# Attention and experts on one core: query rows in another order, a wider ring of banks at the end, activation tables loaded ahead

## What is computed

```python
xn = _layernorm(x, axis=-1)
# attention
q = (x @ w_q.T).reshape(B, S, N_HEADS, dk)
k = x @ w_k.T
v = x @ w_v.T
scores = jnp.einsum('bshd,btd->bhst', q, k) * softmax_scale[0]
attn = jax.nn.softmax(scores, axis=-1)
out = jnp.einsum('bhst,btd->bshd', attn, v).reshape(B, S, D)
return out @ w_out.T
# experts, two of eight for each token
t = (x * jax.lax.rsqrt(ms + EPS) * norm_scale).reshape(Bx * Sx, Dx)
h = _swiglu(t @ w1 + b1)
y = h @ w2 + b2
# together
x = x + s * g
```

## Time and profile before

| | us |
|---|---|
| median of 3 runs | 433.36 (432.69 to 433.53) |
| the profiled execution | 432.73 |
| its span in the trace | 430.9 |
| PE busy | 380.3 (88%) |
| DVE busy | 300.6 (70%) |
| ACT busy | 281.7 (65%) |
| POOL busy | 277.9 (64%) |

### The profile page before, as it was taken

How to read it: one execution, slowest core, us unless ns; L and a number is a source line. 1 busy time by engine, 2 the same in 40 slices (tenths; PEclk the granted TensorE clock), 3 DMA queues, 4 the chain that set the end, 5 groups by cost and what they waited for, 6 DMA issues and landing times.

```text
span 430.9 us, 7859 instructions
## 1 busy us (share of the span) xinstructions
PE 380.3 (88%) x2375; PEld 238.9 (55%) x2375; DVE 300.6 (70%) x559; ACT 281.7 (65%) x615; POOL 277.9 (64%) x417
## 2 busy tenths in 40 slices
PE   1787889898989999999569999989979989999994
PEld 1666655343444445444247988878869854444221
DVE  6678888988897788787515756556546648888532
ACT  4854467666777778677525666656646568887893
POOL 6353053538888888888002888888788882577980
PEclk9999569999999999999958999999999999999998
DMA  6321154562222522322615566666756512535211
GB/s 172 99 86 56 73 194 152 208 258 90 73 100 73 172 86 104 99 82 91 146 33 141 176 200 187 175 183 192 203 149 191 151 46 100 183 118 148 58 44 49
DMA packets 51310, 55.40 MB, mean 129 GB/s; under 512 B 11747, under 2 KB 40291, under 8 KB 51142
## 3 DMA queue, kind: packets, MB, share of 16 engines
q1 hardware_dynamic: 46150, 45.45, 35.2%
q0 software_dynamic: 4544, 9.38, 6.2%
q10 hardware_dynamic: 576, 0.08, 0.1%
HBM read 34.46 MB, written 19.95 MB: 126 GB/s over the span
## 4 chain that ended last, share of the span: by engine, by line
PE 49%; DVE 13%; POOL 13%; ACT 9%; issue 7%; DMA 6%; SPq 2%; ACTq 0%; POOLq 0%; DVEq 0%
PE ps L927 12%; PE ps L899 10%; PE ps L914 10%; POOL y_dram L567 10%; DVE neg L1353 6%; PE ps L1063 6%; POOL kvg L569 3%; ACT probs L754 3%; PE ps L876 2%; PE ps L1086 2%; DMA xs<-sorted_dram 2%; DMA y_dram<-early,xs 2%; DMA b_st<-b_col 2%; PE ps L885 1%; PE ps L974 1%
## 5 line engine op out<-in xcount | busy, mean ns | idle before, releaser
L1353 DVE TENSOR_REDUCE neg<-ps 128x4 f32<-128x1024 f32 x128 | 155.3, 1215 | 39.8 <-PE ps L914 39.6
L754 ACT ACTIVATE probs<-ps 128x512 f32<-128x512 f32 x256 | 141.8, 599 | 37.3 <-PE ps L899 35.0
L567 POOL DMA_INDIRECT y_dram<-early,xs x78 | 77.1, 989 | 52.2 <-ACT early L824 31.3
L899 PE MATMUL ps<-qs,k_stack 96*128 96x512 bf16 x256 | 91.4, 384 | 5.1 <-ACT probs L754 3.3
L914 PE MATMUL ps<-k_stack,qs 93*128 93x256 bf16 x512 | 83.0, 287 | 4.3 <-DVE neg L1353 4.2
L1063 PE MATMUL ps<-early,w_st 128*128 128x256 f32 x312 | 78.3, 396 | 8.0 <-DMA b_st<-b_col 5.9
L1429 DVE TENSOR_SCALAR early<-ps,b_st 128x256 f32<-128x256 f32 x78 | 34.2, 480 | 58.8 <-PE ps L1063 47.2
L542 POOL DMA_INDIRECT sorted_dram<-rows,pos_i x64 | 64.7, 1011 | 11.2 <-POOL rows L537 10.3
L1063 PEld LDWEIGHTS ps<-early,w_st 128*128 128x128 f32 x312 | 58.4, 197 | 17.4 <-issue 10.4
L927 PE MATMUL ps<-probs,v_all 128*32 128x512 f32 x512 | 68.1, 605 | 0.0
L914 PEld LDWEIGHTS ps<-k_stack,qs 93*128 93x128 bf16 x512 | 51.6, 103 | 25.2 <-issue 5.4
(11 more groups left out here) (153 smaller groups left out, 422.9 us busy)
## 6 DMA issues: line engine op xcount, KB each, us to landing
w_st<-in_w SPq DMA_DIRECT2D x39, 256.0 KB
qs<-q_dram SPq DMA_DIRECT2D x32, 288.0 KB
sorted_dram<-s_b SPq DMA_DIRECT2D x10, 520.0 KB, 4.7
xs<-sorted_dram SPq DMA_DIRECT2D x39, 130.0 KB, 2.3
early<-y_dram SPq DMA_DIRECT2D x16, 256.0 KB, 4.2
q_dram<-early SPq DMA_DIRECT2D x16, 192.0 KB, 3.7
rows<-in_x SPq DMA_DIRECT2D x8, 256.0 KB
out<-rows SPq DMA_DIRECT2D x16, 128.0 KB, 2.0
```

Source lines behind the costliest of these rows:

```text
L567: gp.indirect_dma_start(out=y_dram, out_offset=bass.IndirectOffsetOnAxis(ap=at[:, t, :], axis=0), in_=ys[:, r, t, :], in_offset=None).then ...
L754: sc.activation(probs[:, u % 2, k, :], ps[:, bank, :], ACT.Exp).then_inc(m["exp_ok"], 1)
L899: te.matmul(ps[:, bank, :], k_stack[0:KALL, at:at + P], qs[0:KALL, u % QS, j * 512:(j + 1) * 512], start=True, stop=True).then_inc(m["exp_ ...
L1353: ve.tensor_reduce(neg[:, b % 2, st, h:h + 4], ps[:, 3 + 2 * (n % 2):5 + 2 * (n % 2), :].rearrange("p a (e t) -> p (a e) t", e=2), AX, ALU ...
```

## The change

- `load_q`: the dimension of the three copies goes behind the 24 rows (`replicated(..., 3, 1)`), so that the three copies of a source row lie in neighbouring partitions. Same bytes, 72 rows of 4 KB.
- `key_rows`: the three parts of a key are written at every third column instead of as blocks of 24.
- `ring`: from step w = 32 on (WIDE_FROM) the ring has seven banks: the four of the maxima and the old three. Its first four items wait until the last maximum has been read (`max_ok` at 128), the next three on the last three items of the old ring, later ones on the item seven before.
- `values(31, 0)` moves from step u = 32 to step u = 31, between `scores_exp(31, 5)` and `project(14)`.
- ACT: a one-column Silu at q = -1, before the first `L817`, and a one-column Exp at q = 39, before the last two blocks are taken out.

```diff
+WIDE_FROM = len(FIRST_ITEMS) + sum(len(ring_items(w)) for w in range(UNITS))
+WIDE_BANKS = (3, 4, 5, 6, WIDE_FROM % 3, (WIDE_FROM + 1) % 3, (WIDE_FROM + 2) % 3)
+def ring_bank(item):
+    i = RING_NO[item]
+    return i % 3 if i < WIDE_FROM else WIDE_BANKS[(i - WIDE_FROM) % 7]
...
-                sp.dma_start(qs[0:KROWS, u % QS, :], replicated(src[:, (u % 2) * UCOLS:(u % 2 + 1) * UCOLS], 3, 0)
+                sp.dma_start(qs[0:KROWS, u % QS, :], replicated(src[:, (u % 2) * UCOLS:(u % 2 + 1) * UCOLS], 3, 1)
...
+                if q == -1:
+                    sc.activation(root1[:, :], ones_f[:, 0:1], ACT.Silu)
+                if q == BLOCKS:
+                    sc.activation(root1[:, :], ones_f[:, 0:1], ACT.Exp)
...
-                if i >= 3:
+                j = i - WIDE_FROM
+                if j >= 7:
+                    pe.wait_ge(*released(i - 7))
+                elif j >= 4:
+                    pe.wait_ge(*released(WIDE_FROM - 3 + j - 4))
+                elif j >= 0:
+                    pe.wait_ge(m["max_ok"], 4 * UNITS)
+                elif i >= 3:
                     pe.wait_ge(*released(i - 3))
...
-                if 1 <= u <= UNITS:
+                if 1 <= u < UNITS:
                     values(u - 1, 0)
...
+                if u == UNITS - 1:
+                    values(u, 0)
                 if turned:
                     project((u - 3) // 2)
...
-                part = [k_rows[:, a:a + n, 3 * jj * DK:3 * (jj + 1) * DK].rearrange("p t (i d) -> p t i d", i=3) for jj in range(3)]
+                part = [k_rows[:, a:a + n, 0:KROWS].rearrange("p t (i d j) -> p t i d j", i=3, j=3)[:, :, :, :, jj] for jj in range(3)]
```

23 lines of the change are left out of this document (11 added, 12 removed).

## The result

The kernel after takes 430.79 us (median of 20 runs, 424.63 to 434.79) beside 433.71 us for the kernel before in the same comparison; the ratio is 0.986 with an interval of 0.983 to 0.990. Two later comparisons of the same kernel gave 0.994 (0.990 to 0.997) and 0.994 (0.991 to 0.998). The 0.986 leaves out every run more than 1.5% above the fastest of its kernel, which here are ten of the twenty of the changed kernel (one of them took only 424.63 us) and none of the kernel before; the two medians by themselves have a ratio of 0.993. So the change brings 0.6 to 0.7%, 2.5 to 2.9 us, where 2.5% was forecast; 422.7 us and the whole range up to 427.5 were too low.

The account below looks back on a forecast made before the run. The first sorted rows' landing, then POOL's scatters in the experts and ACT in the last four units, were taken as bounds; 432.73 - 9.4 - 0.1 - 0.6 - 0.5 = 422.1 profiled, 422.7 forecast against 433.36, range 418.8 to 427.5.

Parts of the forecast that it names:

- Term 4: Early stage: shorter query loads let POOL's 39.0 us split run at 32.5, ending its collision with DVE; gain 0.5 us.
- rival (d): Early stage: moved splits keep DVE busy, PE's clock stays at 1.2 GHz; slower, 434.5 us; chance 0.04.
- Term 1: Before the experts: query loads spread over twelve engines land the first rows 6.0 us earlier, POOL's first scatter 9.4 us earlier.
- clock row of 214 to 218: Sign at the experts' start: PE's granted clock stays at 1.00 and all L1063 take about 1.9 us.
- Rival (a): Experts' start: PE's clock falls anyway, losing 3.8 us of the query-load gain; 426.5 us, chance 0.12.
- Term 2: ACT's table loads moved ahead: Silu no further gain, Exp before the last two blocks are taken out gains 0.1 us.
- Term 3: Last four units: wide ring recovers 1.7 us of ACT's idle time, loses 0.5 and 0.6; net gain 0.6 us.
- rival (c): Key rows written in strided columns cost 3.5 us at most; 426.2 us, chance 0.04.

Follow-up runs that it names:

- held split and fillers: Changed kernel with POOL's last query split waiting for DVE's third set of maxima parts, plus 8 and 3 unread matmuls at the experts' start: 422.43 us, ratio 0.981.
- third profile of after: The changed kernel run again unaltered, beside the kernel before at 430.68 us on one chip: 428.15 us, ratio 0.994 to before.
- filler, second: Changed kernel with unread matmuls on PE, 10 while it waits for the first rows and 3 behind the first turn, second run: 426.93 us, ratio 0.991.
- the fillers: Changed kernel with unread matmuls on PE at the experts' start (10 and 3): first run 426.25 us, ratio 0.990 to before; second 426.93 us, 0.991.
- ring only: Kernel before with the seven banks and the moved values alone: 431.78 us, ratio 1.002 to before.
- values back: Changed kernel with values(31, 0) at its old place behind project, seven banks kept: 423.63 us, one run.
- the rows first: First sorted-row loads issued ahead of the two query loads; here on the changed kernel with last split held and 9 unread matmuls: 421.40 against 432.11 us, ratio 0.974.
- the held split: Changed kernel with POOL's last query split waiting for DVE's third set of maxima parts: 423.54 us, ratio 0.983, beside the changed kernel's 428.15 us.
- held split, the first: First run of the changed kernel with POOL's last query split waiting for DVE's third set of maxima parts: 431.38 against 438.20 us, ratio 0.983.

## Why the prediction was wrong

**The bound** was read rightly, in the main. The wait for the first rows and POOL's first scatter set the time of the end: with held split and fillers the first scatter is at 224.74, the prediction wanted it "at about 224", and that kernel takes 8.3 us less than the one before. In the third profile of after and the other three kernels of its chip the scatters' stretch is 123.3 to 123.9 us wherever it begins, so the lead is carried whole. It isn't the same in all series: 124.7 to 127.9 in four kernels on another chip, 126.3 to 127.6 in four on a third, the kernel with nothing but the tables among them, and 125.7 in the first profile of after, where it swallows 2.1 of the 5.84 us won. The third chip gave 124.1 and 123.5 in a later series, so it isn't the chip either. PE's waits for b_st differ in place and length from profile to profile. That is not of the change; what sets it is open.

**Term 4, the early stage, is the step that failed.** The prediction moved the split of 39 us and took the later one for a split that "hardly moves". The step behind it: each write on SP stands behind query loads, so every later split moves too, the last one by 6.9 us, while DVE's program around it came forward by 3.5 (L1360 at 76.09 against 79.62). In the changed kernel's other two profiles the split moved by 3.9 and 4.5 us and met L1360 just the same. The bounds named the danger, a lost microsecond "if the moved split meets other work of DVE", and rival (d) had the engine and the direction, but it was dismissed by looking at one split alone. It was priced at under 1 us or a whole unit; it costs 4.6 us by the medians. In the first profile 1.5 us of DVE's time is seen directly. Most of the rest goes by PE's clock, 2.6 us for each fall: it was down at some time between 79 and 91 us in all eight profiles with the spread and the split free, in three of the twelve others. In two of those eight it fell again at 102 to 110 us. That the collision brings the fall about is likely by these counts, not shown, since it also came without. What was predicted of the split at 39 us came true: the copy of 96 columns takes 0.20 us in after instead of 0.72, and `load_m(0)` comes 0.5 us sooner in two of the three profiles.

The Trainium skill (SBUF — State Buffer, "Who interferes with whom") states why the two meet: a VectorE instruction with two inputs in SBUF shares a port with a GpSimd instruction that reads SBUF, whoever starts first keeps it to the end, and `tensor_reduce` doesn't take part. The traces agree: L1360 ends with POOL's L512 (77.23 and 77.19), L1267 0.27 us after L516, and the L1373 between them takes its usual 1.21 us. In the one profile with 0.59 us (filler, second) the DVE instruction just before, a `tensor_tensor` of 0.42 us, took 1.39 beside L512, and PE's wait was 2.12 us.

**Term 1.** The direction and twelve engines were right, and the landing came 4.85 us sooner after its issue, where 6.0 was forecast: a load needs 1.75 us, so an engine moves its share at about half the rate that it has as one of three. This is 1.1 us mis-sized, and the term's 9.4 us were 5.84 at the first scatter. That the clock row of 214 to 218 "stays at 1.00" failed: it fell at a pause of PE of 2.38 us (2.17 and 2.23 in the other two profiles). Rival (a) had a chance of 0.12 and was what happened. Its 3.8 us fit one profile of three: from the first turn to the first scatter the changed kernel takes 13.6, 15.5 and 12.9 us, with the fillers 11.3, so slow blocks cost 1.6 to 4.2. In the mean only 1.2 come back with the fillers, which also put the turn 0.9 us later behind the last probs. The one-column Silu starts at 214.03, 0.02 us after the load's end, so the 1.28 us of the earlier trace rows were the right price. The further 1.38 us that the Trainium skill (ScalarE: Activation LUTs, "What ACT_TABLE_LOAD costs") states for a drain are not seen. But the start was not late by the table: the rows landed after it.

**Term 2.** Exp came out about as reckoned: the load stands at 343.65, PE's wait of 0.15 us is gone, and from PE's return to DVE's last maximum there are 47.2 to 47.3 us with the tables ahead and 47.5 without, 0.2 instead of 0.1. Nothing of Silu is measurable.

**Term 3** was right in size, and its parts went the way that was predicted: 0.5 lost at the first wide scores (0.24 + 0.39 measured), the 0.43 of o_T stays (it does), 0.6 of stall before `s` 14 (0.82), 1.7 recovered (the rows with 0.72, 0.27, 0.72 are gone). These measured parts make only 0.3 together. From the start of DVE's last maximum to the end of ACT's last `probs` there are 24.5 us in the four profiles without the ring, 23.9 in the fifteen with the ring and the moved values, ring only among them: 0.6 as forecast. So half of it comes from ACT's instructions following each other more closely, which the prediction didn't have, and the exact sum is in part luck. With the values back it is 23.0, so the ring alone is worth 1.5 and the move costs 0.9, by one profile. The lines of that stretch, values back (DVE's and ACT's timelines):

```profile
390.05 1.23 DVE L1371 TENSOR_REDUCE neg<-ps 128x4 f32<-128x1024 f32 x1 [0.17 <-PE ps L932]
...
411.89 1.12 ACT L761 ACTIVATE probs<-ps 128x512 f32<-128x512 f32 x2
```

And ring only:

```profile
397.82 1.23 DVE L1369 TENSOR_REDUCE neg<-ps 128x4 f32<-128x1024 f32 x1 [0.17 <-PE ps L928]
...
420.62 1.08 ACT L761 ACTIVATE probs<-ps 128x512 f32<-128x512 f32 x2
```

Behind the last `probs` come 8.8 to 10.0 us, which differ from profile to profile whatever the kernel; that is why the last column of the table doesn't show the 0.6 in each row.

**The strided keys**, rival (c): the first cast of 384 elements went from 0.58 to 0.73 us, the second stayed at 0.74, the subtraction behind it went from 0.67 to 0.80: 0.3 us for the largest call, well below the doubling.

The forecast gain was 10.7 us; the change by itself had 2.5 to 2.9. With the split held, the fillers in and the rows first, the chip shows 10.7 us too (432.11 less 421.40), but that is luck: this kernel has three things that the prediction didn't count on. Of the missing 8 us the held split accounts for 4.6, the fillers for perhaps 1.2, the slower loads for 1.1; the rest stays open.

## What to carry to other kernels

A faster transfer moves all that waits for it, on every engine. Walk the whole row of waiters to its end, and look at each new neighbour, above all where VectorE and GpSimd come to stand side by side on a path that TensorE waits for. Where a transfer lands late because it is queued, ask first whether it could be issued earlier: a changed order on SP did here what a new layout was meant to do, and left POOL's splits and DVE's work beside each other as they were.

## What the runs showed of the hardware

- A VectorE instruction of 0.18 us with two SBUF inputs took 1.14 us beside a GpSimd `tensor_tensor` in seven of eight profiles (0.59 in the eighth, where the instruction before it was held up instead, 1.39 us for 0.42), 0.18 or 0.19 in the twelve in which the two didn't meet. Reductions out of PSUM between them were not slowed.
- A 288 KB load in 72 rows of 4 KB moves at 74 GB/s on three engines and needs 1.75 us on twelve, about 14 GB/s an engine instead of 25; some other packets ran beside it.
- TensorE's granted clock fell to 0.50 after pauses of 1.7 to 2.5 us, but also at 82 to 90 us in two executions whose longest pause before it was 0.74 us, and it stayed up in one profile with a pause of 1.78 us (held split, the first). A fall of 6.8 us at 80 to 90 us cost 2.6 us (`load_m(1)` to `load_m(3)`, 33.2 instead of 30.6). A single profile doesn't tell what a change does to the clock; the mean over many executions does. It stayed up at the experts' start in all seven profiles of kernels with nine to thirteen matmuls of 512 columns there.
